# Down products of the gated experts as three f16 products, and no forced dense stretch before a step of the recurrence

## The chip, the cores and the metric

The kernel runs on one core of one Trainium2 chip. The metric is device time in microseconds, the median of several executions; the kernel before took 1439.15 us (three runs, 1434.42 to 1448.94).

## What is computed

Two decoder layers over x of 2 x 1024 tokens and 256 features. Each layer adds three results to x, each from a layer norm of x. Layer 0: causal self-attention (16 heads of 16), cross-attention to 77 context rows, and a mixture of 8 linear experts. Layer 1: a recurrence over the 1024 tokens, cross-attention, and a gated mixture of experts.

```
# the recurrence of layer 1, one step for each token
h_new = tanh(xt + h @ Wh.T + bh)

# the gated mixture of layer 1 (16 routed experts of 64, shared part of 512)
combine = zeros(S, E); combine[token, top 4 experts] = w
g = einsum('sc,ech->esh', xf, gate_w)
u = einsum('sc,ech->esh', xf, up_w)
h = silu(g) * u
hw = h * combine.T[:, :, None]
routed = einsum('esh,ehc->sc', hw, down_w)
out = x + shared_out + routed
```

The shared part has the same form without `combine`. Both parts stand side by side in the kernel as 1536 hidden features: 12 blocks of 128, of which 4 are shared and 8 routed.

## The kernel before, in words

**Chunks.** The tokens are cut into four chunks of 512 columns (256 tokens of each of the two sequences). Every layer works chunk by chunk; chunk c of a layer needs chunk c of the layer before, and the recurrence makes the history in order of time, 256 steps for a chunk.

**The recurrence.** A step is: TensorE `hi` (8 products of 2 columns, line 515), then `lo` (4 products, line 515); ScalarE `tanh` twice (line 560 to f16, line 561 to f32); VectorE `sub` (line 566), which makes the low half. `lo` waits for `sub`, `hi` of the next step for the first tanh. The 1023 steps are one chain through three engines. All other work of the layers is put between the pieces of that chain: the recurrence of chunk 0 starts when layer 0 has done its first chunk, and everything later runs beside it.

**The order.** No engine picks its work at run time. `Plan.make` writes the order of each engine before the kernel is built, from a table of costs (the number in each `st.add`), and holds a piece back that would delay the next piece of the chain by more than an allowance. Where TensorE would wait in the plan, it puts in `idle` products (line 534, up to 512 columns each, result unused). `burst` adds to that: in front of `hi` number 127, 255, ... (every `BURST_STEPS` = 128) the plan makes TensorE run for at least `BURST` = 1.7 us without a gap, with `idle` products where there is no other work.

**The gated experts.** For each of the 48 blocks (4 chunks x 12): TensorE `make` (12 products of 512 columns, line 1611, f16 pairs: high x high, low x high, high x low, for gate and up), ScalarE `tanh` (line 1619), VectorE `silu` (line 1624) and `product` (line 1632) into `hT` (a ring of three, in `tail`); for routed blocks TensorE `spread` (line 1640) and VectorE `weigh` (line 1648); then TensorE `down`: four f32 products of 256 columns (line 1663), 192 over the kernel. The program gives each f32 product to the engine as two instructions, so the profile counts 384. After 12 blocks VectorE `update` (line 1671) adds the sums to x, and `store` writes x out. The router's choice of experts is 32 short VectorE instructions for a chunk (`route`, lines 1525 to 1594). The gate and up weights are loaded in f32 and split into a high and a low f16 half in 8 parts (lines 1919 and 1924); the down weights stay in f32 in `vp`.

Of the kernel before, what the change touches and what calls it, by code (L numbers as in the profile page):

```python
# [9 lines left out]
F16 = mybir.dt.float16  # L10
# [160 lines left out]
LEAST_GAP = 0.1  # L171
BURST_STEPS = 128
BURST = 1.7
# [1245 lines left out]
class GatedExperts:  # L1419
# [7 lines left out]
    def __init__(self, st, w, ln, rank, out, room):  # L1427
        self.st, self.g, self.w, self.ln, self.room_in = st, st.g, w, ln, room.room_in
        self.xh, self.xl, self.hT, self.th = room.xh, room.xl, room.hT, room.th
        self.ex, self.sc, self.sx, self.sel, self.comb = (room.gates[:, k] for k in range(5))  # L1430
# [4 lines left out]
        self.ov = out.rearrange("(t p) d -> p t d", p=P)  # L1435
        self.s = st.sems("gat", "xh xl logits ex chain cT cph cpl cleared made th sv hm spread hc down fx stored")
        n = NK
# [27 lines left out]
        st.add("v", "gat_hc", self.weigh, n * NR, 0.66, lambda i: rank(i // NR) + 0.24, closes=lambda i: ("gat_s", i))  # L1465
        st.add("pe", "gat_down", self.down, n * MH * TC, 0.43, lambda i: rank(i // (MH * TC)) + 0.25,
               opens=lambda i: ("gat_d", i // (MH * TC), i % TC // 2) if i // TC % MH == 0 and i % 2 == 0 else None)
# [159 lines left out]
    def product(self, v, i):  # L1627
        v.wait_ge(self.s["sv"], i + 1)
        v.wait_ge(self.s["made"], 2 * i + 2)
        if i >= 3:  # L1630
            v.wait_ge(self.s["down"], i - 2)
        v.scalar_tensor_tensor(out=self.hT[:, i % 3, :], in0=self.th[:, i % 3, :], scalar=0.5 / LIFT ** 2,
                               in1=self.st.bank("gat", 2 * i + 1)[:], op0=ALU.mult, op1=ALU.mult
                               ).then_inc(self.s["hm"], 1)
# [8 lines left out]
    def weigh(self, v, i):  # L1643
# [5 lines left out]
                        ).then_inc(self.s["hc"], 1)  # L1649

    def down(self, pe, i):
        c, m, p = i // (MH * TC), i // TC % MH, i % TC
        n = MH * c + m
        o = self.st.bank("gat_d", c, p // 2)
        if m == 0 and p % 2 == 0:
            o = self.st.take(pe, "gat_d", c, p // 2)
        if i == 0:
            pe.wait_ge(*self.w.gated_in)
        if p == 0 and m < MS:
            pe.wait_ge(self.s["hm"], n + 1)  # L1660
        if p == 0 and m >= MS:
            pe.wait_ge(self.s["hc"], NR * c + m - MS + 1)
        last = pe.matmul(o[:, D * (p % 2):D * (p % 2) + D], self.hT[:, n % 3, P * p:P * p + P], self.w.wd[:, m, :],  # L1663
                         start=m == 0 and p % 2 == 0, stop=m == MH - 1, skip_group_check=True)
        if p == TC - 1:
            last.then_inc(self.s["down"], 1)

    def update(self, v, j):
        x, p = self.g.x[:, tile_of(j)[3], :], column(j) // P
        v.wait_ge(self.s["down"], MH * (j // TC + 1))  # L1670
        v.tensor_tensor(x, self.st.bank("gat_d", j // TC, p // 2)[:, D * (p % 2):D * (p % 2) + D], x, ALU.add
                        ).then_inc(self.s["fx"], 1)

# [9 lines left out]
def all_layers(g, a, out):  # L1683

    with ExitStack() as ctx:
# [24 lines left out]
        whole = tail[:].rearrange("p (k n) -> p k n", k=KD)  # L1710
        gated_room.hT = tail[:, 0:1536].rearrange("p (a n) -> p a n", a=3)
        gated_room.th = tail[:, 1536:3072].rearrange("p (a n) -> p a n", a=3)
        gated_room.xh = vp[:, 3072:3584].bitcast(F16).rearrange("p (k n) -> p k n", k=KD)
# [49 lines left out]
        wx1.ctx_in, wx1.q_in, wx1.w_in = (s["ctx1_in"], 80), (s["q1_in"], 64), (s["q1_in"], 64)  # L1763
        w.wd, w.w_hi, w.w_lo = vp[:, 0:3072].rearrange("p (m n) -> p m n", m=MH), w_parts[0:2], w_parts[2:4]
        w.gated_in = (s["w_in"], 48)
# [114 lines left out]
        def load_second(sp, i):  # L1880
# [14 lines left out]
            if i == 2:  # L1895
# [3 lines left out]
                sp.dma_start(w.cb, a["cbias"].partition_broadcast(P)).then_inc(s["w_in"], 16)  # L1899
                sp.dma_start(w.wd, a["down"].rearrange("(m p) n -> p m n", p=P)).then_inc(s["w_in"], 16)  # L1900

# [11 lines left out]
        def part(i):  # L1913
            return slice(i % 4 * HID // 4, (i % 4 + 1) * HID // 4)

        def split_high(act, i):
            j = i // 4
            act.wait_ge(s["whole_in"], 16 * (j + 1))
            act.activation(w.w_hi[j][:, :, part(i)], whole[:, :, part(i)], ACT.Copy, scale=LIFT).then_inc(s["whole_high"], 1)

        def split_low(v, i):
            j = i // 4
            v.wait_ge(s["whole_high"], i + 1)
            v.scalar_tensor_tensor(out=w.w_lo[j][:, :, part(i)], in0=whole[:, :, part(i)], scalar=LIFT,
                                   in1=w.w_hi[j][:, :, part(i)], op0=ALU.mult, op1=ALU.subtract
# [112 lines left out]
        st.add("act", "lift", lift, 1, 0.5, lambda i: -2000)  # L2038
        st.add("act", "split_high", split_high, 8, 0.8, lambda i: 1000)
        st.add("v", "split_low", split_low, 8, 0.85, lambda i: 1000)  # L2040
        st.add("v", "router", router, 2, 0.2, lambda i: 1000)
# [72 lines left out]
```

## Time and profile before

| | |
|---|---|
| median of 3 runs | 1439.15 us (1434.42 to 1448.94) |
| the profiled execution | 1442.69 us, of which the span is 1440.9 us |
| TensorE busy | 1390.5 us (96%), 19662 matmuls |
| VectorE, ScalarE busy | 814.0 us (56%), 598.6 us (42%) |
| first and last tanh of the recurrence | 223.46 us and 1299.14 us |
| mean granted TensorE clock | 0.974 |

The first 223 us are layer 0 of chunk 0 and the starts of chunk 1. Then come 1075.7 us of recurrence with other work beside it, and a tail of 141.8 us in which the recurrence is over: cross-attention of the last chunk and the gated experts of the last two. A product of TensorE is shown with its latency, so a row of one product of 256 columns says 0.27 us and a row of several in a sequence says less for each. In a row of the timeline the first number is the start, the second the time from the first start to the last end.

### The profile page before, as it was taken

How to read it: one execution, taken by the hardware profiler on the slowest of the kernel's cores; microseconds unless marked ns; L12 is line 12 of the kernel's file. 1: busy time of each engine (PE TensorE's matmuls, PEld its weight loads, DVE VectorE, ACT ScalarE, POOL GpSimd, SP SyncE). 2: the span in 40 equal slices, each digit the busy share in tenths (PEclk: the TensorE clock that was granted, in tenths of full speed). 3: DMA queues.
4: the chain of work that ended last, by engine and by line, in shares of the span. 5: the costliest groups of instructions: out<-in, count | busy, mean ns of one | idle time of the engine just before them, and what ended most of it. 6: DMA issues, size and time to landing. Idle time of an engine off the chain costs nothing.

```text
span 1440.9 us, 48024 instructions
## 1 busy us (share of the span) xinstructions
PE 1390.5 (96%) x19662; PEld 948.9 (66%) x19662; DVE 814.0 (56%) x2606; ACT 598.6 (42%) x2786; POOL 38.1 (3%) x60
## 2 busy tenths in 40 slices
PE   5699889999999999999999999999999999999998
PEld 4466346777757777775676777675766676766655
DVE  6746873278774227878841227757444553347473
ACT  2072315733424783342278864451523324332310
POOL 2000000000000000000000001000000000000000
PEclk9799989999999999999999999999989999989999
DMA  5654100030000003110000003210000200002000
GB/s 160 90 141 92 54 1 3 8 58 3 3 3 3 3 3 56 23 25 3 3 4 3 3 3 133 55 24 2 2 2 17 39 3 2 17 2 38 2 15 15
DMA packets 45469, 40.18 MB, mean 28 GB/s; under 512 B 9723, under 2 KB 44486, under 8 KB 45254
## 3 DMA queue, kind: packets, MB, share of 16 engines
q1 hardware_dynamic: 43526, 36.32, 11.4%
q8 instruction: 160, 2.62, 0.8%
q10 hardware_dynamic: 1728, 0.79, 0.5%
q14 instruction: 55, 0.45, 0.1%
HBM read 25.81 MB, written 10.80 MB: 25 GB/s over the span
## 4 chain that ended last, share of the span: by engine, by line
PE 92%; DVE 5%; DMA 1%; ACT 1%; SPq 0%; issue 0%; DVEq 0%; ACTq 0%
PE b L515 22%; PE b L1611 9%; PE b L534 8%; PE b L1663 7%; PE b L1390 6%; PE b L1003 6%; PE b L974 5%; PE b L740 4%; PE b L696 3%; PE b L919 3%; DVE mx L928 3%; PE b L1259 2%; PE b L1234 2%; PE b L651 2%; PE b L459 2%; PE b L501 1%
## 5 line engine op out<-in xcount | busy, mean ns | idle before, releaser
L515 PEld LDWEIGHTS b<-hp,whp 128*128 128x128 f16 x12276 | 476.1, 96 | 266.9 <-ACT hp L560 168.1
L515 PE MATMUL b<-hp,whp 128*128 128x2 f16 x12276 | 536.5, 165 | 1.6 <-ACT hp L560 0.3
L566 DVE TENSOR_TENSOR hp<-hist,hp 128x4 f16<-128x4 f32 x1023 | 164.7, 161 | 448.2 <-ACT hist L561 439.1
L560 ACT ACTIVATE hp<-b 128x4 f16<-128x4 f32 x1024 | 178.0, 174 | 484.4 <-PE b L515 473.5
L928 DVE TENSOR_REDUCE mx<-b 128x1 f32<-128x512 f32 (+3 forms) x304 | 187.5, 652 | 0.9 <-PE b L922 0.7
L988 ACT ACTIVATE vp<-b 128x512 f32<-128x512 f32 x288 | 171.6, 601 | 19.4 <-PE b L977 11.8
L561 ACT ACTIVATE hist<-b 128x4 f32<-128x4 f32 x1024 | 177.1, 173 | 0.0
L1611 PE MATMUL b<-vp,heads 128*128 128x512 f16 x576 | 160.1, 381 | 0.0
L534 PE MATMUL b<-whp 128*128 128x512 f16 (+6 forms) x586 | 157.9, 346 | 0.0
L919 PE MATMUL b<-heads 128*128 128x512 f16 (+3 forms) x384 | 111.8, 329 | 5.4 <-DVE mx L928 2.2
L1663 PE MATMUL b<-vp,tail 128*128 128x256 f32 x384 | 112.9, 404 | 0.0
L1390 PE MATMUL b<-we,xT 128*128 128x512 f16 x384 | 106.1, 383 | 0.0
L974 PE MATMUL b<-heads 128*128 128x256 f16 (+1 forms) x640 | 100.9, 263 | 2.0 <-DMA heads<-mp 1.8
L1003 PE MATMUL b<-vp 128*32 128x256 f32 (+1 forms) x1280 | 95.4, 370 | 0.0
L1245 ACT ACTIVATE x_pr<-b 77x512 f32<-77x512 f32 x128 | 72.8, 592 | 26.9 <-PE b L1234 26.0
L1415 DVE SCALAR_TENSOR_TENSOR x<-b,wts,x 128x256 f32<-128x256 f32 x128 | 61.8, 483 | 23.7 <-PE b L1390 18.5
L1611 PEld LDWEIGHTS b<-vp,heads 128*128 128x128 f16 x576 | 49.5, 97 | 30.4 <-ACT x_osb L645 0.5
L1663 PEld LDWEIGHTS b<-vp,tail 128*128 128x128 f32 x384 | 64.0, 191 | 8.1 <-issue 3.2
L445 POOL TENSOR_TENSOR rs<-ve,neg_half 128x2 f32<-128x2 f32 x48 | 33.8, 705 | 1334.2 <-DVE ve L439 1334.2
L974 PEld LDWEIGHTS b<-heads 128*128 128x128 f16 x640 | 55.1, 97 | 11.4 <-issue 4.7
L1619 ACT ACTIVATE tail<-b 128x512 f32<-128x512 f32 x48 | 28.7, 599 | 77.6 <-PE b L1611 77.6
L1204 DVE TENSOR_REDUCE x_nm<-b 128x4 f32<-128x308 f32 x128 | 56.8, 472 | 1.4 <-PE b L1195 0.7
(213 smaller groups left out, 1566.9 us busy)
## 6 DMA issues: line engine op xcount, KB each, us to landing
x_qs<-qx_scr SPq DMA_DIRECT2D x48, 128.0 KB
qx_scr<-xq_pair SPq DMA_DIRECT2D x16, 256.0 KB, 2.1
heads<-q_scr SPq DMA_DIRECT2D x24, 128.0 KB, 4.4
heads<-k_scr SPq DMA_DIRECT2D x36, 64.0 KB, 2.5
x<-in_x SPq DMA_DIRECT2D x8, 256.0 KB, 7.3
q_scr<-tail SPq DMA_DIRECT2D x8, 256.0 KB, 2.3
k_scr<-tail SPq DMA_DIRECT2D x8, 256.0 KB, 2.3
x_qs<-in_L_ffn_We SPq DMA_DIRECT2D x2, 1024.0 KB, 6.0
```

The lines of the kernel that those rows point to most:

```text
L515: return pe.matmul(self.z(t)[:, m], self.w.whp[:, a, k, m * P:(m + 1) * P], self.g.hp16[:, (t - 1) % 2, part, k, :], start=False, stop=Tru ...
L534: pe.matmul(self.g.b7[:, 0:min(512, columns - at)], self.w.whp[:, 0, 0, 0:P], self.w.whp[:].rearrange("p a k n -> p (a k n)")[:, 0:min(512 ...
L560: act.activation(self.g.hp16[:, t % 2, 0], self.z(t), ACT.Tanh, scale=1 / LIFT).then_inc(self.s["hi_ready"], 1)
L561: act.activation(self.g.hist[:, :, :, t % (4 * HALF)], self.z(t), ACT.Tanh, scale=1 / LIFT).then_inc(self.s["full_ready"], 1)
L566: v.tensor_tensor(self.g.hp16[:, t % 2, 1], self.g.hist[:, :, :, t % (4 * HALF)], self.g.hp16[:, t % 2, 0], ALU.subtract).then_inc(self.s[ ...
L928: v.tensor_reduce(self.mx[:, column(j) // P, head:head + heads, int(first > 0)], self.st.bank("self_first", i)[:, 0:P * n * heads].rearran ...
L974: last = pe.matmul(o[:, N * e:N * e + N], self.ks[:, b, h // 2, P * kb:P * kb + P], self.qs[:, h, QW * b + first:QW * b + QW], start=True, ...
L988: act.activation(self.pr[:, n % 2, e0:e0 + heads, first:QW], self.st.bank("self_s", i)[:, 0:N * heads].rearrange("p (e n) -> p e n", e=hea ...
L1003: last = pe.matmul(o[QD * e:QD * e + QD, QW * b + first:QW * b + QW], self.va[:, b * (S // P) + kb, at:at + QD], self.pr[:, n % 2, e, firs ...
L1390: last = pe.matmul(o[:], x[:, k, column(j):column(j) + P], self.w.we[:, wt, k, D * e:D * e + 2 * D], start=at == 0, stop=at == self.PER - 1)
L1611: last = pe.matmul(o[:], wt[:, k, m * P:(m + 1) * P], x[:, k, :], start=at == 0, stop=at == 5)
L1663: last = pe.matmul(o[:, D * (p % 2):D * (p % 2) + D], self.hT[:, n % 3, P * p:P * p + P], self.w.wd[:, m, :], start=m == 0 and p % 2 == 0, ...
```

## The change

Two parts. `BURST_STEPS` is 1024, so no `hi` of the 1023 has the forced stretch in front of it. And the down products take f16 pairs: the down weights are loaded to `heads` and split in 4 parts (ScalarE high, VectorE low), each finished hidden block is split by ScalarE (`keep_hidden`) and VectorE (`hidden_low`), and each of the 192 down products is a sum of three f16 products of 256 columns. The sum is 64 times too large (`LIFT`), which `update` takes back.

```diff
-BURST_STEPS = 128
+BURST_STEPS = 1024
...
         st.add("v", "gat_hc", self.weigh, n * NR, 0.66, lambda i: rank(i // NR) + 0.24, closes=lambda i: ("gat_s", i))
-        st.add("pe", "gat_down", self.down, n * MH * TC, 0.43, lambda i: rank(i // (MH * TC)) + 0.25,
+        st.add("act", "gat_hh", self.keep_hidden, n * MH, 0.52, of_block(0.245))
+        st.add("v", "gat_hl", self.hidden_low, n * MH, 0.6, of_block(0.246))
+        st.add("pe", "gat_down", self.down, n * MH * TC, 0.33, lambda i: rank(i // (MH * TC)) + 0.25,
...
         if i >= 3:
-            v.wait_ge(self.s["down"], i - 2)
+            v.wait_ge(self.s["hl"], i - 2)
...
+    def keep_hidden(self, act, n):
+        c, m = self.blocks[n]
+        if m < MS:
+            act.wait_ge(self.s["hm"], n + 1)
+        else:
+            act.wait_ge(self.s["hc"], NR * c + m - MS + 1)
+        if n >= 3:
+            act.wait_ge(self.s["down"], n - 2)
+        act.activation(self.hp[:, n % 3, 0, :], self.hT[:, n % 3, :], ACT.Copy).then_inc(self.s["hh"], 1)
+
+    def hidden_low(self, v, n):
+        v.wait_ge(self.s["hh"], n + 1)
+        v.tensor_tensor(self.hp[:, n % 3, 1, :], self.hT[:, n % 3, :], self.hp[:, n % 3, 0, :], ALU.subtract
+                        ).then_inc(self.s["hl"], 1)
...
-        if p == 0 and m < MS:
-            pe.wait_ge(self.s["hm"], n + 1)
-        if p == 0 and m >= MS:
-            pe.wait_ge(self.s["hc"], NR * c + m - MS + 1)
-        last = pe.matmul(o[:, D * (p % 2):D * (p % 2) + D], self.hT[:, n % 3, P * p:P * p + P], self.w.wd[:, m, :],
-                         start=m == 0 and p % 2 == 0, stop=m == MH - 1, skip_group_check=True)
+        if i == 0:
+            pe.wait_ge(self.w.s["whole_split"], 12)
+        if p == 0:
+            pe.wait_ge(self.s["hl"], n + 1)
+        for at, (h, wd) in enumerate(((0, self.w.wd_hi), (0, self.w.wd_lo), (1, self.w.wd_hi))):
+            last = pe.matmul(o[:, D * (p % 2):D * (p % 2) + D], self.hp[:, n % 3, h, P * p:P * p + P], wd[:, m, :],
+                             start=m == 0 and p % 2 == 0 and at == 0, stop=m == MH - 1 and at == 2, skip_group_check=True)
...
-        v.tensor_tensor(x, self.st.bank("gat_d", j // TC, p // 2)[:, D * (p % 2):D * (p % 2) + D], x, ALU.add
-                        ).then_inc(self.s["fx"], 1)
+        v.scalar_tensor_tensor(out=x, in0=self.st.bank("gat_d", j // TC, p // 2)[:, D * (p % 2):D * (p % 2) + D],
+                               scalar=1 / LIFT, in1=x, op0=ALU.mult, op1=ALU.add).then_inc(self.s["fx"], 1)
...
-                sp.dma_start(w.wd, a["down"].rearrange("(m p) n -> p m n", p=P)).then_inc(s["w_in"], 16)
+                sp.dma_start(wd_whole, a["down"].rearrange("(m p) n -> p m n", p=P)).then_inc(s["w_in"], 16)
...
+            if j == 2:
+                act.wait_ge(*w.gated_in)
+                act.activation(w.wd_hi[:, wd_part(i)], wd_whole[:, wd_part(i)], ACT.Copy, scale=LIFT
+                               ).then_inc(s["whole_high"], 1)
+                return
...
-        st.add("act", "split_high", split_high, 8, 0.8, lambda i: 1000)
-        st.add("v", "split_low", split_low, 8, 0.85, lambda i: 1000)
+        st.add("act", "split_high", split_high, 12, 0.8, lambda i: 1000)
+        st.add("v", "split_low", split_low, 12, 0.85, lambda i: 1000)
```

Since the plan is made anew, work moves on every engine from step 126 on (line numbers of the changed kernel from 1500 on are 2 to 34 higher: 1613 is `make`, 1642 `spread`, 1681 `down`, 1650 `weigh`, 1661 `keep_hidden`, 1665 `hidden_low`).

The first place is TensorE in front of `hi` number 127 (a row of line 515 is a `hi` of 8 products or a `lo` of 4, or both in a row of 12), before:

```order
L515 MATMUL b<-hp,whp 128x2 x8
L919 MATMUL b<-heads 128x512
L515 MATMUL b<-hp,whp 128x2 x4
L534 MATMUL b<-whp 128x512 x7
L534 MATMUL b<-whp 128x320
L515 MATMUL b<-hp,whp 128x2 x12
L1234 MATMUL b<-x_qs,x_ks 77x256 x4
```

and with the change:

```order
L515 MATMUL b<-hp,whp 128x2 x8
L919 MATMUL b<-heads 128x512
L515 MATMUL b<-hp,whp 128x2 x4
L534 MATMUL b<-whp 128x512
L534 MATMUL b<-whp 128x384
L515 MATMUL b<-hp,whp 128x2 x8
L919 MATMUL b<-heads 128x512
```

The run of 3904 idle columns in front of the step has become one of 896 columns, as in the steps around it.

The second place is TensorE in the last chunk of the gated experts, around the turning of the router's weights (line 1582, with the change 1584), before:

```order
L1611 MATMUL b<-vp,heads 128x512 x5
L1582 MATMUL b<-ident,vp 16x128 x4
L1611 MATMUL b<-vp,heads 128x512 x7
L1663 MATMUL b<-vp,tail 128x256
L1640 MATMUL b<-mp,sel_pair 128x512
L1663 MATMUL b<-vp,tail 128x256
L1640 MATMUL b<-mp,sel_pair 128x512
L1663 MATMUL b<-vp,tail 128x256 x2
L1611 MATMUL b<-vp,heads 128x512 x12
```

and with the change:

```order
L1613 MATMUL b<-vp,heads 128x512 x8
L1584 MATMUL b<-ident,vp 16x128 x4
L1613 MATMUL b<-vp,heads 128x512 x4
L534 MATMUL b<-whp 128x512 x3
L1642 MATMUL b<-mp,sel_pair 128x512 x2
L534 MATMUL b<-whp 128x512
L1642 MATMUL b<-mp,sel_pair 128x512
L534 MATMUL b<-whp 128x512 x10
L534 MATMUL b<-whp 128x256
L1681 MATMUL b<-vp,heads 128x256 x12
```

Where useful products stood between the router and the next down products, 14 idle products of 512 columns and one of 256 stand now.

The third place is VectorE in the same chunk, where routed blocks follow one another: `silu`, `product`, `weigh` before,

```order
L1624 SCALAR_TENSOR_TENSOR tail<-tail,b 128x512
L1632 SCALAR_TENSOR_TENSOR tail<-tail,b 128x512
L1648 TENSOR_TENSOR tail<-tail,b 128x512 x2
L1624 SCALAR_TENSOR_TENSOR tail<-tail,b 128x512
L1632 SCALAR_TENSOR_TENSOR tail<-tail,b 128x512
```

and with the change, with `hidden_low` behind them:

```order
L1634 SCALAR_TENSOR_TENSOR tail<-tail,b 128x512
L1650 TENSOR_TENSOR tail<-tail,b 128x512 x3
L1665 TENSOR_TENSOR heads<-tail,heads 128x512 x3
L1626 SCALAR_TENSOR_TENSOR tail<-tail,b 128x512
L1634 SCALAR_TENSOR_TENSOR tail<-tail,b 128x512
```

Each block has one VectorE instruction more in front of its down products, and three of them stand in a row behind the router.

## Rows read from the trace of the kernel before

**Rows 1.** The page, part 1: busy time, share of the span, instructions.
```profile
PE 1390.5 (96%) x19662; PEld 948.9 (66%) x19662; DVE 814.0 (56%) x2606; ACT 598.6 (42%) x2786; POOL 38.1 (3%) x60
```

**Rows 2.** Waits: engine, line, waited for, us in total, times, longest.
```profile
ACT hp L560 <- PE b L515: 473.5, 693, 2.4
DVE hp L566 <- ACT hist L561: 439.1, 687, 3.2
PEld b L515 <- ACT hp L560: 168.1, 525, 0.6
```

**Rows 3.** Groups by line and form, whole span: busy us, mean ns, idle before.
```profile
L1611 PE MATMUL b<-vp,heads 128*128 128x512 f16 x576 | 160.1, 381 | 0.0
L974 PE MATMUL b<-heads 128*128 128x256 f16 x512 | 83.4, 274 | 2.0 <-DMA heads<-mp 1.8
L1648 DVE TENSOR_TENSOR tail<-tail,b 128x512 f32<-128x512 f32 x32 | 21.6, 686 | 0.2
L1857 ACT ACTIVATE we<-x_qs 128x512 f16<-128x512 f32 x8 | 4.8, 629 | 0.0
```

**Rows 4.** Timeline of ScalarE around step 128: start, us, line.
```profile
346.79 0.17 ACT L560 ACTIVATE hp<-b 128x4 f16<-128x4 f32 x1 [0.69 <-PE b L515]
347.73 0.17 ACT L560 ACTIVATE hp<-b 128x4 f16<-128x4 f32 x1 [0.69 <-PE b L515]
349.68 0.17 ACT L560 ACTIVATE hp<-b 128x4 f16<-128x4 f32 x1 [1.70 <-PE b L515]
```

**Rows 5.** Timeline of ScalarE around step 896.
```profile
1171.14 0.17 ACT L560 ACTIVATE hp<-b 128x4 f16<-128x4 f32 x1 [0.54 <-PE b L515]
1173.06 0.17 ACT L560 ACTIVATE hp<-b 128x4 f16<-128x4 f32 x1 [1.68 <-PE b L515]
```

**Rows 6.** Timeline of TensorE, two f16 products of 256 columns in a row.
```profile
236.77 0.38 PE L974 MATMUL b<-heads 128*128 128x256 f16 x2
```

**Rows 7.** Timeline in the tail: `down` and `make` of one block, and the end.
```profile
1412.02 1.99 PE L1663 MATMUL b<-vp,tail 128*128 128x256 f32 x8
1413.85 2.75 PE L1611 MATMUL b<-vp,heads 128*128 128x512 f16 x12
...
1431.36 5.45 PE L1663 MATMUL b<-vp,tail 128*128 128x256 f32 x24
1431.92 0.69 DVE L1648 TENSOR_TENSOR tail<-tail,b 128x512 f32<-128x512 f32 x1
1436.84 1.42 DVE L1671 TENSOR_TENSOR x<-b,x 128x256 f32<-128x256 f32 x4 [4.23 <-PE b L1663]
```

**Rows 8.** Busy time by stretch: us; PE, PEld, DVE, ACT, POOL; clock, DMA, GB/s.
```profile
1277.80:1299.10 21.30, 20.97 (x383) 13.59 (x381) 10.91 (x48) 8.16 (x54) 0.69 (x1) 1.00 0.01 3
...
1380.00:1410.00 30.00, 29.89 (x142) 16.86 (x143) 22.51 (x51) 4.87 (x9) 0.00 (x0) 1.00 0.00 1
```

**Rows 9.** TensorE by stretch: busy and count, granted clock.
```profile
223.50:349.70 126.20, 126.20 (x2305) 1.00 0.12 20
...
1069.50:1072.90 3.40, 3.40 (x40) 1.00 0.02 5
1072.90:1083.20 10.30, 10.30 (x79) 0.50 0.00 0
...
1264.10:1277.70 13.60, 13.60 (x149) 0.50 0.01 2
```

**Rows 10.** Timeline of ScalarE, one step that holds other work.
```profile
946.36 0.17 ACT L560 ACTIVATE hp<-b 128x4 f16<-128x4 f32 x1 [0.24 <-PE b L515]
946.61 0.59 ACT L1245 ACTIVATE x_pr<-b 77x512 f32<-77x512 f32 x1
947.14 0.17 ACT L560 ACTIVATE hp<-b 128x4 f16<-128x4 f32 x1
```

**Rows 11.** Timeline of TensorE, step 740: its `hi` and its `lo`.
```profile
964.63 0.34 PE L515 MATMUL b<-hp,whp 128*128 128x2 f16 x8
...
1000.76 0.24 PE L515 MATMUL b<-hp,whp 128*128 128x2 f16 x4
```

More of the change, by code:

```diff
@@ L1428, in __init__ @@
         self.st, self.g, self.w, self.ln, self.room_in = st, st.g, w, ln, room.room_in
-        self.xh, self.xl, self.hT, self.th = room.xh, room.xl, room.hT, room.th
+        self.xh, self.xl, self.hT, self.th, self.hp = room.xh, room.xl, room.hT, room.th, room.hp
         self.ex, self.sc, self.sx, self.sel, self.comb = (room.gates[:, k] for k in range(5))
@@ L1435, in __init__ @@
         self.ov = out.rearrange("(t p) d -> p t d", p=P)
-        self.s = st.sems("gat", "xh xl logits ex chain cT cph cpl cleared made th sv hm spread hc down fx stored")
+        self.s = st.sems("gat", "xh xl logits ex chain cT cph cpl cleared made th sv hm spread hc hh hl down fx stored")
         n = NK
@@ L1711, in all_layers @@
         gated_room.hT = tail[:, 0:1536].rearrange("p (a n) -> p a n", a=3)
+        gated_room.hp = heads[:, 9216:10752].bitcast(F16).rearrange("p (a b n) -> p a b n", a=3, b=2)
+        wd_whole = heads[:, 6144:9216].rearrange("p (m n) -> p m n", m=MH)
         gated_room.th = tail[:, 1536:3072].rearrange("p (a n) -> p a n", a=3)
@@ L1763, in all_layers @@
         wx1.ctx_in, wx1.q_in, wx1.w_in = (s["ctx1_in"], 80), (s["q1_in"], 64), (s["q1_in"], 64)
-        w.wd, w.w_hi, w.w_lo = vp[:, 0:3072].rearrange("p (m n) -> p m n", m=MH), w_parts[0:2], w_parts[2:4]
+        w.wd_hi, w.wd_lo = (vp[:, 1536 * k:1536 * k + 1536].bitcast(F16).rearrange("p (m n) -> p m n", m=MH) for k in range(2))
+        w.w_hi, w.w_lo = w_parts[0:2], w_parts[2:4]
         w.gated_in = (s["w_in"], 48)
@@ L1914, in part, with wd_part @@
             return slice(i % 4 * HID // 4, (i % 4 + 1) * HID // 4)
+        def wd_part(i):
+            return slice(i % 4 * MH // 4, (i % 4 + 1) * MH // 4)
         def split_high(act, i):
             j = i // 4
+            if j == 2:
[3 more added lines that the diff above has]
+                return
             act.wait_ge(s["whole_in"], 16 * (j + 1))
@@ L1923, in split_low @@
             v.wait_ge(s["whole_high"], i + 1)
+            if j == 2:
+                v.scalar_tensor_tensor(out=w.wd_lo[:, wd_part(i)], in0=wd_whole[:, wd_part(i)], scalar=LIFT,
+                                       in1=w.wd_hi[:, wd_part(i)], op0=ALU.mult, op1=ALU.subtract
+                                       ).then_inc(s["whole_split"], 1)
+                return
             v.scalar_tensor_tensor(out=w.w_lo[j][:, :, part(i)], in0=whole[:, :, part(i)], scalar=LIFT,
```

## The prediction

> **What bounds the kernel now.** I read the page's busy times first: TensorE is busy 96% of the span, VectorE 56%, ScalarE 42% [rows 1]. So the cause of the time is on TensorE, but not as work alone, since it also runs idle products. The waits show the second limit: in 525 of 1023 steps TensorE's weight load waited for the first tanh, 168.1 us together; ScalarE waited 473.5 us for TensorE and VectorE 439.1 us for the second tanh [rows 2]. The kernel is in about half of its steps bound by the chain and in the other half by what TensorE was given between the pieces. In the tail (1299 to 1441 us) there is no chain; TensorE is busy 29.89 of 30 us in the stretch 1380 to 1410 [rows 8], so there each product removed counts in full unless its place is filled again.
>
> **The forced stretches.** The step into tanh 128 took 349.68 - 347.73 = 1.95 us, the one before it 0.94 us [rows 4]. The step into tanh 896 took 1.92 us [rows 5]; steps around it take 0.79. There are seven such steps (128, 256, ..., 896), the other five 1.69 to 1.94 us long. Removing them gives 1.0 us each: **-7.1 us**, all on the chain, since in the row of the order the idle columns (3904 of them at the first) are what TensorE does there.
>
> **The down products, price.** One f32 product: a block's four start at 1412.02, the next `make` at 1413.85 [rows 7], so 0.457 us each. Two f16 products of 256 columns take 0.38 us from start to end, one takes 0.274 [rows 3, 6], so 0.106 us apart, and by the `down` sequence of the change 3 x 0.108 = 0.325 us for a sum of three (0.108 is half of the 0.216 at which products of 512 columns follow: (2.75 - 0.381) / 11, [rows 3, 7]). Saved: 0.132 us a product, 192 of them, 25 us of TensorE, if nothing else moved.
>
> **The down products, place.** By the order, 96 of the 192 are before the last step, 96 behind it, before as after.
> - In steps: of the 96, 8 stand before and 10 with the change in the long stretch of step 740. That stretch is a hole in the chain, `hi` at 964.63, `lo` at 1000.76 [rows 11]; the change does not remove it, in spite of its words. In it 8 x 0.457 turn into 10 x 0.325 (-0.4) and idle columns rise by 5504 (+2.3), other products by +0.3: **+2.2 us**. The remaining 88 save 0.132 each, but only where TensorE and not the chain sets the step: half, **-5.8 us**. Nine `make` products (0.216 each) go from the steps to the tail: **-1.9 us**.
> - New work of ScalarE and VectorE in steps: 25 splits of a block on each. ScalarE's nearest row is 0.629 us (f32 to f16, 512 wide), VectorE's 0.686 [rows 3]; the weights add 4 parts of 768 columns on each, at 1.03 us by their width (0.686 x 1.5, the dearer row). These stand in the queues of tanh and `sub`. Lower bound of the cost: nothing. A step of 0.78 us holds a ScalarE instruction of 0.59 us without delay [rows 10]. Upper bound: each its whole length, 25 x (0.629 + 0.686) + 8 x 1.03 = +41 us. Between, ScalarE is idle 473.5 / 1023 = 0.46 us and VectorE 0.43 us a step [rows 2], so 25 x (0.17 + 0.26) + 4 x (0.57 + 0.60) = +15 us if every such step were a shortest one. The row of a real step is nearest to nothing, and half of the steps have more room: I take **+1 us**.
>
> Sum in the steps: -7.1 + 2.2 - 5.8 - 1.9 + 1 = -11.6 us.
>
> **The tail.** -12.7 us for 96 down products, +1.9 us for the nine `make`, and idle columns go from 14400 to 36352, which at 0.216 us for 512 are **+9.3 us**. They stand in front of places where the plan sees VectorE late: per block it has 0.686 us more (`hidden_low`). In 1380 to 1410 us VectorE works 22.51 us [rows 8]; eight more instructions make it 28.0 of 30 us, so it is nearly the bound there, and I add **+1 us** for what the plan's 0.60 us does not have of 0.686. The end: before, the last 24 instructions run from 1431.36 to 1436.8; with the change the last block's `weigh` ends at 1431.92 + 0.69 = 1432.6 [rows 7], the splits follow (0.63 + 0.69 and some 0.15 of signals: 1434.1), then 12 products of 0.108 (1435.4 and latency 0.17, so 1435.6): **-1.2 us**, of which the products before (1431.36 + 24 x 0.108 = 1433.95) hide the rest. But that gain is already in the -12.7, so it isn't added. The four `update` instructions at the very end are chained by one another's 0.36 us and grow by 0.07 each: +0.2. Sum in the tail: -0.3 us.
>
> Total **-12 us**: span and execution go from 1440.9 and 1442.69 us to 1429 and 1430.7. The profiled execution is 3.5 us above the median of the runs, within their spread of 14.5 us, so I take the same -12 off the median: **1427 us**.
>
> **The clock, where row and rule part.** The granted clock was at its lower level, 1.2 GHz, from 1072.9 to 1083.2 and from 1264.1 to 1277.7 us (and twice more, for 6.8 us each) although TensorE was busy all of these stretches, 10.30 of 10.30 us in the first [rows 9]. In the second it gave 149 products in 13.6 us, 11.0 a us; right behind it 383 in 21.3 us, 18.0 a us [rows 8, 9]: 5.3 us lost. Before that first fall it had no gap either, 3.40 of 3.40 us, but only 40 matmuls in it, 11.8 a us against 18.3 a us in the first 126 us of steps [rows 9]. The Trainium skill, TensorE: Matmul & The Clock Gate, section Loop structure matters more than you think, has the clock fall where TensorE waits long between groups of matmuls; by that rule a kernel that never stops TensorE pays nothing, and neither do the stretches removed here: the clock's term of the sum would be 0 by the rule. By the rows it can be something. I take 0 all the same, from other rows: from 223.5 to 349.7 us no forced stretch had yet run, and the clock stayed at 2.4 GHz (1.00) throughout [rows 9].
>
> **Rivals.**
> 1. *The saved time is given back in waits* (the chain takes all that isn't a forced stretch). For it: 525 steps wait for tanh. Against it: the other half do not. Only the -7.1 remain, with +2.2 in the hole and +1 for queues: 1439 - 4 = 1435 us. Chance 0.22.
> 2. *The plan uses all of it.* If the counted columns set the time everywhere, the steps give -12.7 (96 products) - 1.9 (`make`) and, for idle columns, which fall from 227776 to 223424, -1.8, so -16.4; the tail -1.5: 1421 us. For it: TensorE is busy 99.8% in the steps. Against: busy counts latency. Chance 0.24.
> 3. *The clock falls instead* (slower than before). The mechanism is thin work that no dense stretch interrupts: TensorE in front of steps 128 to 896. If the clock fell once in each of the seven spans from which a stretch is gone, at 5.3 us each, +37 us: 1464 us. It decides from the third such fall on (3 x 5.3 is more than 12). For it: four falls in the rows with TensorE busy. Against: none in the first 126 us, without a stretch. Chance 0.08.
> 4. *The new queue work delays the chain by the average shortage*, +15 for +1: 1441 us, no change. It would need the splits to stand in the shortest steps. Chance 0.06.
>
> My forecast, -12 us give or take 5, has 0.40.
>
> **How the numbers follow.** The predicted time is the likeliest case's, 1427 us, its own range 1421 to 1433. The range for 8 in 10 reaches on the fast side past rival 2 to one clock stretch less than before (1421 - 5 - 2 = 1414), on the slow side over rival 1 and up to rival 4's middle, with one clock stretch more (1435 + 5): 1440. A measurement of this kernel can tell about 1% (14.4 us), so faster is below 1424.8 us: most of rival 2 (0.20) and the faster half of the forecast's own spread, with runs that differ by 14.5 us (0.21): 0.41. Slower is above 1453.5 us: 0.08 of rival 3 and 0.02 of the others: 0.10. The rest, 0.49, is within 1%.
>
> **What the changed profile would show.** Steps into tanh 128, 256, ... of 0.8 to 1.1 us (burst term right); a step 740 of some 39 us; `down` in groups of 12 that take 1.3 us up to the next `make`, against 1.83 (price right); mean of VectorE's new line near 0.69 and of ScalarE's near 0.63 us; first to last tanh near 1064 us, against 1075.7 (sum in the steps); from the last tanh to the end about 141.5 us (tail). More than 45 us at the lower clock would speak for rival 3, steps around the new splits longer by 0.2 us or more for rival 4. The prediction is wrong if the tail grows by more than 3 us through VectorE, or if the order's new packing lets waits of other kinds (transfers, stores of the cross-attention) stand in front of a step.

## The result, and the profile after

The changed kernel took 1423.83 us, the median of four runs (1419.4 to 1426.8), beside 1437.69 us for the kernel before: a ratio of 0.9877, 95% interval 0.9836 to 0.9918. The forecast was 1427 us; its range, 1414 to 1440, holds the time. The whole interval lies below 1, so the direction was right. The size was forecast too small: by the ratio the kernel gained 17.7 us (0.0123 x 1437.69), by the two medians alone 13.9 us, where the forecast had 12. At equal clock, as explained with the table below, it is 18 us.

The page of the changed kernel, part 1 (the row of [rows 1] is its counterpart):

```profile
span 1422.8 us, 48634 instructions
PE 1374.9 (97%) x19892; PEld 938.5 (66%) x19892; DVE 845.1 (59%) x2658; ACT 626.7 (44%) x2838; POOL 37.9 (3%) x60
```

TensorE stays the bound; VectorE works 31 us and ScalarE 28 us more, mainly for the splits. The waits (engine, line, waited for: us in total, times, longest), beside [rows 2]:

```profile
ACT hp L560 <- PE b L515: 433.6, 672, 1.5
DVE hp L566 <- ACT hist L561: 402.1, 673, 3.2
PEld b L515 <- ACT hp L560: 170.8, 537, 0.4
```

ScalarE and VectorE wait 40 and 37 us less for the chain, while TensorE's own wait for tanh hardly moves (168.1 before). The steps became shorter because TensorE had less to do between them, not because the chain itself did. Groups by line and form (busy us, mean ns, idle before), beside [rows 3]:

```profile
L1681 PE MATMUL b<-vp,heads 128*128 128x256 f16 x576 | 78.7, 272 | 0.0
L1665 DVE TENSOR_TENSOR heads<-tail,heads 128x512 f16<-128x512 f32 x48 | 32.5, 686 | 6.2 <-ACT heads L1661 6.1
L1689 DVE SCALAR_TENSOR_TENSOR x<-b,x 128x256 f32<-128x256 f32 x16 | 6.2, 418 | 3.4 <-PE b L1681 3.4
L1661 ACT ACTIVATE heads<-tail 128x512 f16<-128x512 f32 x48 | 30.0, 630 | 23.6 <-DVE tail L1650 17.2 <-DVE tail L1634 6.4
```

The prices of the split instructions are those of the forecast (forecast 0.686 and 0.629 us, measured 0.686 and 0.630). The `update` has not grown by the forecast's 0.07 us: it takes 0.418 us, as before.

ScalarE's timeline around step 128 and step 896 of the changed kernel (start, us, line), the counterparts of [rows 4, 5]:

```profile
349.42 0.17 ACT L560 ACTIVATE hp<-b 128x4 f16<-128x4 f32 x1 [0.69 <-PE b L515]
350.35 0.17 ACT L560 ACTIVATE hp<-b 128x4 f16<-128x4 f32 x1 [0.69 <-PE b L515]
...
1161.67 0.17 ACT L560 ACTIVATE hp<-b 128x4 f16<-128x4 f32 x1 [0.54 <-PE b L515]
1162.49 0.17 ACT L560 ACTIVATE hp<-b 128x4 f16<-128x4 f32 x1 [0.57 <-PE b L515]
```

The step into tanh 128 takes 0.93 us, it took 1.95; the one into tanh 896 takes 0.82, it took 1.92. Now the stretches of the span, from the starts of line 560 in each trace (the start of a trace varies by 5 us between kernels with the same first 200 us, and means nothing):

| | before | changed | difference | forecast |
|---|---|---|---|---|
| tanh 0 to tanh 640, no gated experts in them | 634.3 | 632.7 | -1.7 | -5.1 |
| the long step 740 | 36.75 | 39.26 | +2.5 | +2.2 |
| the other steps from 640 on | 404.6 | 384.3 | -20.3 | -8.7 |
| last tanh to the end | 141.8 | 141.4 | -0.4 | -0.3 |

The forecast's column is its own sum, cut at step 640: five and two forced stretches (-5.1, -2.0), then -5.8, -1.9 and +1. One row is wrong by much: the steps with gated experts. The clock is in these rows too. Both profiles have 37.5 us at the lower clock between the first and the last tanh, but before has all of it from step 640 on, and the changed kernel has 3.4 us in front of it and 34.1 us behind. At the forecast's rate (5.3 us lost in 13.6) that moves 1.3 us from one row to the other: at equal clock the first row is -3.0 and the third -19.0. The second profile of the changed kernel, without a fall in front of step 640, says 631.2 us for the first row, -3.1.

### The profile page after: what moved, and what is told of

It reads as the page before. It is cut to its first block, busy times and chain, and to the rows that moved or that the text cites. A ratio compares the mean times of both kernels' runs of the same rounds, so it can differ in the third digit from the quotient of the medians.

```text
span 1422.8 us, 48634 instructions
## 1 busy us (share of the span) xinstructions
PE 1374.9 (97%) x19892; PEld 938.5 (66%) x19892; DVE 845.1 (59%) x2658; ACT 626.7 (44%) x2838; POOL 37.9 (3%) x60
## 4 chain that ended last, share of the span: by engine, by line
PE 92%; DVE 4%; DMA 1%; ACT 1%; issue 1%; SPq 0%; DVEq 0%; ACTq 0%
PE b L515 23%; PE b L1613 9%; PE b L534 8%; PE b L1390 6%; PE b L1003 6%; PE b L974 5%; PE b L740 5%; PE b L1681 5%; PE b L919 4%; PE b L696 3%; DVE mx L928 3%; PE b L1259 3%; PE b L1234 2%; PE b L651 2%; PE b L459 2%; PE b L501 1%
## 5 line engine op out<-in xcount | busy, mean ns | idle before, releaser
L534 PE MATMUL b<-whp 128*128 128x512 f16 (+6 forms) x624 | 168.8, 347 | 0.0
L1681 PE MATMUL b<-vp,heads 128*128 128x256 f16 x576 | 78.7, 272 | 0.0
L1613 PEld LDWEIGHTS b<-vp,heads 128*128 128x128 f16 x576 | 50.0, 97 | 29.8 <-issue 0.7
L974 PEld LDWEIGHTS b<-heads 128*128 128x128 f16 x640 | 55.0, 97 | 11.4 <-issue 4.6
L1681 PEld LDWEIGHTS b<-vp,heads 128*128 128x128 f16 x576 | 51.2, 97 | 10.1 <-issue 2.3
L919 PEld LDWEIGHTS b<-heads 128*128 128x128 f16 x384 | 36.5, 97 | 29.2 <-DVE mx L928 22.2
```

Of the source, the lines that this page charges most:

```text
L534: pe.matmul(self.g.b7[:, 0:min(512, columns - at)], self.w.whp[:, 0, 0, 0:P], self.w.whp[:].rearrange("p a k n -> p (a k n)")[:, 0:min(512 ...
L919: last = pe.matmul(o[:, at:at + P * n], self.qs[:, h, column(j):column(j) + P], self.ks[:, b, h // 2, P * first:P * first + P * n], start= ...
L974: last = pe.matmul(o[:, N * e:N * e + N], self.ks[:, b, h // 2, P * kb:P * kb + P], self.qs[:, h, QW * b + first:QW * b + QW], start=True, ...
L1613: last = pe.matmul(o[:], wt[:, k, m * P:(m + 1) * P], x[:, k, :], start=at == 0, stop=at == 5)
L1681: last = pe.matmul(o[:, D * (p % 2):D * (p % 2) + D], self.hp[:, n % 3, h, P * p:P * p + P], wd[:, m, :], start=m == 0 and p % 2 == 0 and ...
```

## The experiments

The runs of one kernel differ by more than most of the effects, and each run lists its mean granted clock. Over all 163 executions in the 14 rows of the table (the changed kernel has two) straight lines with one slope fit with a scatter of 1.5 us: 1.08 us less for each 0.001 of clock. The last two columns are worked out with it: a kernel's time at a clock of 0.977, against the kernel before at the same clock. Where medians and this column differ, the kernel ran at another mean clock. The runs were made in three groups, each beside its own runs of before; these come out at 1438.3, 1437.5 and 1437.2 us at a clock of 0.977, so a difference between kernels of different groups is good to about 1 us and no better.

| kernel | median, us | ratio to before, 95% | mean clock | at 0.977, us | difference |
|---|---|---|---|---|---|
| before (60 runs) | 1436.7 to 1445.1 | | 0.9747 | 1437.7 | |
| changed (4 runs) | 1423.83 | 0.9877 [0.9836, 0.9918] | 0.9735 | 1419.7 | -18.0 |
| changed, again | 1422.83 | 0.9899 [0.9863, 0.9934] | 0.9730 | 1420.0 | -17.7 |
| no stretches, f32 | 1434.0 | 0.9946 [0.9916, 0.9976] | 0.9775 | 1433.8 | -3.9 |
| stretches, f16 pairs | 1419.75 | 0.9855 [0.9813, 0.9897] | 0.9808 | 1422.9 | -14.8 |
| f16 products alone, old order | 1414.5 | 0.9834 [0.9788, 0.9879] | 0.9757 | 1413.9 | -23.8 |
| splits alone | 1442.33 | 1.0031 [0.9997, 1.0065] | 0.9764 | 1442.8 | +5.1 |
| stretches every 64 steps | 1433.78 | 0.9958 [0.9923, 0.9992] | 0.9742 | 1429.6 | -8.1 |
| router filled | 1424.87 | 0.9890 [0.9844, 0.9937] | 0.9742 | 1420.5 | -17.2 |
| router and bias filled | 1416.58 | 0.9836 [0.9792, 0.9879] | 0.9835 | 1423.4 | -14.3 |
| measured durations in the table | 1432.0 | 0.9925 [0.9887, 0.9962] | 0.9685 | 1420.7 | -17.0 |
| allowance 0.35 | 1413.81 | 0.9812 [0.9757, 0.9867] | 0.9745 | 1412.0 | -25.7 |
| no low half | 1422.24 | 0.9869 [0.9814, 0.9923] | 0.9710 | 1415.8 | -21.9 |
| both fills, measured durations | 1419.13 | 0.9845 [0.9793, 0.9898] | 0.9820 | 1424.8 | -12.9 |

### The two parts apart

Without the forced stretches, everything else as before:

```diff
-BURST_STEPS = 128
+BURST_STEPS = 1024
```

> The kernel before with the forced stretches alone taken out (f32 down products stay). Theory A (the forecast's term): seven steps shorter by 1.0 us each, all on the chain: 7 us less, 1430 to 1431 us. Rival B (given back): in the changed kernel the seven steps are 7.0 us shorter together, but steps 0 to 640, where five of them lie and nothing else of the change does, took 632.6 us against 634.3 us, only 1.7 us less; then this kernel gains 2 to 3 us, 1435 us. Rival C (clock): without the stretches the granted clock falls more often; slower than before, with more than 45 us at the lower clock.

7.8 us less by the ratio, 3.9 at equal clock. Steps 0 to 640 took 631.3 us against 634.3: -3.0, where the five steps with a stretch became 4.9 us shorter (4.5 us together, 9.4 before). The plan that is made anew lengthened the other steps by 1.9 us. It gave back more at the end: from the last tanh on the kernel took 146.0 us against 141.8, though no stretch ever stood there. Step 740 is 2.2 us shorter, and the other steps from 640 on are 6.8 us shorter, of which the clock has 4.0 (27.3 us at the lower clock against 37.5). The four places make -3.0 - 2.2 - 2.8 + 4.2 = -3.8 us. Rival B is what happened at equal clock; the 7 us of theory A are within the interval of the ratio only with the clock's help.

The changed kernel with the stretches back:

```diff
-BURST_STEPS = 1024
+BURST_STEPS = 128
```

> The changed kernel with the forced stretches put back (every 128 steps). Theory A: what the forecast left for the f16 products, -5 us against before (1433 us). Theory D (the f16 products are worth more than forecast, since an f32 product costs 0.515 us between the pieces of a step and not 0.457): the changed kernel's -17.7 us less the 2 to 7 us of the stretches, so -11 to -15 us: 1423 to 1427 us.

-14.8 us at equal clock: theory D. And -3.9 - 14.8 = -18.7 against -18.0 and -17.7 for both: the parts add up within the 1 us of the groups. The places do not add up so simply: with the stretches the tail takes 135.7 us and step 740 takes 42.34, in the changed kernel 141.4 and 39.26. Taking the stretches out lengthens the tail here too, by 5.7 us. By its median alone this kernel is as fast as the changed one or faster, and that is the clock: 0.9808 against 0.973.

### What the f16 products are worth

The order of before, with the products exchanged and nothing added on the other engines:

```diff
-        last = pe.matmul(o[:, D * (p % 2):D * (p % 2) + D], self.hT[:, n % 3, P * p:P * p + P], self.w.wd[:, m, :],
+        for at in range(3):
+            last = pe.matmul(o[:, D * (p % 2):D * (p % 2) + D], self.w.w_lo[at // 2][:, at % 2, P * p:P * p + P],
```

> The order of the kernel before, instruction for instruction, with each f32 down product replaced by three f16 products of 256 columns on other resident operands; no splits of the hidden block, no new plan. It leaves out the use of the hidden block and of the down weights. Theory A (0.132 us saved a product, half of it lost in steps): 1 + 5.8 in the steps and 12.7 in the tail, -19.5 us: 1418 us. Theory D (in steps a product starts behind products of 2 columns, and takes 0.515 us; the three take 0.325): 88 x 0.19 + 1 + 12.7, up to -30 us where TensorE sets every such step: 1408 to 1413 us; first to last tanh 12 to 18 us shorter than 1075.7.

-23.8 us at equal clock, between the two. By stretches of the profile: tail 132.0 us against 141.8 (-9.8), step 740 -0.75, the other steps from 640 on 386.0 against 404.6 (-18.6). In those steps this run had 17 us less at the lower clock than the profiled run of before (20.5 against 37.5), worth 6.6 us at the 5.3 us lost in 13.6 of the forecast. That leaves -12.0 us for 88 products: 0.136 us each, where the forecast put 0.066. A comparison step by step needs no correction, since both kernels have the same order: the steps in which the clock was at its upper level in both profiles, with 85 of the products in 73 of them, became 11.4 us shorter, 0.134 us for a product; the 271 other steps changed by 0.0 us in sum.

The rows say why. TensorE's timeline in a step of before:

```profile
963.91 0.34 PE L515 MATMUL b<-hp,whp 128*128 128x2 f16 x8
964.11 0.68 PE L1663 MATMUL b<-vp,tail 128*128 128x256 f32 x2
```

The `lo` or `hi` behind it starts at 964.63 [rows 11], 0.52 us after the product did. In a step of the changed kernel:

```profile
1033.13 0.49 PE L1681 MATMUL b<-vp,heads 128*128 128x256 f16 x3
1033.46 0.44 PE L515 MATMUL b<-hp,whp 128*128 128x2 f16 x12
```

0.33 us. Of the single f32 products in steps that have a chain product behind them, the median of this distance is 0.515 us. The difference lies between the two instructions of a pair. In a stream of f32 products each instruction starts 0.216 us after the one before. The first pair of a stream is further apart, the more so the shorter the product in front of it: 0.299 us behind products of 2 columns, which follow one another by 0.025 us, 0.258 behind 154 columns, 0.218 behind 256 and 0.216 behind the 512 of `make`. That fits a weight load (0.19 us for f32, 0.097 for f16) that only a long enough product in front can cover. Behind `spread` (48 rows), where the load starts with its own product and not ahead of it, it is 0.320:

```profile
1412.02 1.59 PEld L1663 LDWEIGHTS b<-vp,tail 128*128 128x128 f32 x8 [0.23 <-issue]
```

So the forecast's 0.457 was (0.320 + 7 x 0.216) / 4; a block's four products behind `make` take 0.432 each. Saved in a step is therefore up to 0.19 us and not 0.132, and of at most 88 x 0.19 = 16.7 us the chain takes back some 5 us, not half of 11.6.

### What the splits cost

The kernel before, with `keep_hidden` and `hidden_low` added and waited for, f32 products as they were:

```diff
+        st.add("act", "gat_hh", self.keep_hidden, n * MH, 0.52, of_block(0.245))
+        st.add("v", "gat_hl", self.hidden_low, n * MH, 0.6, of_block(0.246))
...
-        if p == 0 and m < MS:
-            pe.wait_ge(self.s["hm"], n + 1)
+        if p == 0:
+            pe.wait_ge(self.s["hl"], n + 1)
```

> The kernel before (forced stretches stay, down products in f32) with the two split instructions of each hidden block added and waited for; their results are not used. Theory A (the forecast): +1 us in the steps and about +10 us in the tail, where idle columns go from 14400 to 36416: 1448 to 1450 us. Rival E (new work in the queues of tanh and sub delays the chain by its shortage): +11 us more in the steps, first to last tanh 1087 us or more: 1460 us.

+5.1 us at equal clock, less than either. First to last tanh 1074.9 us against 1075.7, the tail 144.2 against 141.8. But this profile has 27.3 us at the lower clock between the tanhs and before has 37.5, worth 4.0 us, so at equal clock the steps are 3.2 us longer. The new work in the queues of tanh and `sub` costs about 3 us there, more than the forecast's 1 and far less than the 15 of its rival 4, which is out; how much of the 3 is a wait in a queue and how much another order was not taken apart. And idle columns that a plan shows in the tail are not all lost time: they went up by 22016, or 9.3 us, and the tail by 2.4 us. They partly stand where TensorE would have waited, or where other work was done earlier.

The changed kernel without VectorE's half:

```diff
-        st.add("v", "gat_hl", self.hidden_low, n * MH, 0.6, of_block(0.246))
...
-        for at, (h, wd) in enumerate(((0, self.w.wd_hi), (0, self.w.wd_lo), (1, self.w.wd_hi))):
+        for at, (h, wd) in enumerate(((0, self.w.wd_hi), (0, self.w.wd_lo), (0, self.w.wd_hi))):
```

> The changed kernel without VectorE's split instruction: the third product takes the high half of the hidden block again, so the low half is left out of the sum. TensorE has the same products. Idle columns in the tail 24064 against 36352 (-5.2 us), in the steps 225280 against 223424 (+0.8). The forecast's terms for this instruction, +9.3 + 1 us of idle columns and VectorE time in the tail and up to +1 in the steps, give -5 to -8 us at equal clock; if the instruction delays the chain (rival 4 of the forecast), -12 us or more.

4 us less than the changed kernel at equal clock, just short of the 5 to 8: the VectorE instruction costs about what the other experiment gave for both. But the gain is not where it was expected: the tail, with 12288 idle columns fewer, took 143.1 us against 141.4, and step 740 took 33.96 against 39.26. The parts put together: -23.8 + 5.1 = -18.7, where f16 pairs as a whole gave -14.8. In step 740 alone f16 pairs as a whole gave +5.6 us where the two parts gave -0.8 and -0.4. The remaining 4 us (splitting the weights, another packing) were not taken apart.

### The forced stretches and the clock

> The changed kernel once more, beside the others of this group. In the runs so far a kernel's time falls by 1.1 us for each 0.001 of mean granted clock, and the changed kernel had 0.9735 in four runs, the one with f16 products and the forced stretches 0.9808. If that difference belongs to the kernels, this comes out at 1423 to 1424 us again with 0.973 to 0.975; if it was the luck of four runs, at 1419 to 1421 us.

It repeats: -17.7 us at equal clock, clock 0.973.

```diff
-BURST_STEPS = 1024
+BURST_STEPS = 64
```

> The changed kernel with forced stretches twice as often as before, every 64 steps (15 of them; plan made anew). Theory A: 1.0 us each without getting anything back: +15 us on the changed kernel. Theory B (part of a stretch is given back by the plan, as 5.1 us in five steps became 3.0 us net in steps 0 to 640): +9 us at equal clock. Theory C (stretches hold the clock up): mean clock 0.98 or more and no more than +3 us.

9.6 us slower than the changed kernel at equal clock, for 15 stretches: 0.64 us each, theory B. Its mean clock is 0.9742. With stretches the means are 0.9747 (before), 0.9808 and 0.9742, without 0.9775, 0.9735 and 0.9730: no order in it. By these means forced stretches at a distance of 64 or 128 steps do not hold the clock, and the fall of rival 3 (slower than before) did not come.

Where the clock falls in the changed kernel (TensorE by stretch: busy and count, granted clock), beside [rows 9]:

```profile
904.50:911.30 6.80, 6.59 (x100) 0.50 0.25 73
911.30:1105.90 194.60, 193.84 (x2831) 1.00 0.05 9
1105.90:1119.50 13.60, 13.60 (x134) 0.50 0.06 20
1252.60:1262.90 10.30, 10.30 (x139) 0.50 0.01 2
```

And what TensorE did before the second and the third of these falls:

```profile
1101.33 0.29 PE L63 MATMUL b<-first,vp 128*128 128x16 f16 x6
1101.73 0.52 PE L515 MATMUL b<-hp,whp 128*128 128x2 f16 x12
1102.11 0.30 PE L63 MATMUL b<-first,vp 128*128 128x16 f16 x6
1102.52 0.52 PE L515 MATMUL b<-hp,whp 128*128 128x2 f16 x12
...
1249.20 0.24 PE L515 MATMUL b<-hp,whp 128*128 128x2 f16 x4
1249.38 0.69 PE L698 MATMUL b<-bo,one_row 1*128 1x256 f32 x2
1250.00 0.45 PE L515 MATMUL b<-hp,whp 128*128 128x2 f16 x12
```

Router products of 16 columns, and bias products with one active row. That is a pattern and not yet a cause, but it is in all profiles: in each of the eleven whose router products have nothing put behind them at least one fall from step 640 on, 17 in all, starts 0.1 to 2.4 us after such a product. Idle products behind the first:

```diff
             for k in range(KD)]).then_inc(self.s["logits"], 1)
+        self.fill(pe)
...
+        gated.fill = lambda pe: rnn.idle(pe, 512)
```

> The changed kernel with one idle product of 512 columns behind each of the 16 groups of router products (16 columns wide) of the gated experts; same order otherwise. Theory F (the clock falls behind thin work, and the falls at 904 and 1106 us follow the router's products): these two falls, 6.8 and 13.7 us long, are gone or shorter, mean clock up by 0.005, 16 x 0.216 = 3.5 us at most are paid and 5 to 8 us come back: 1419 to 1422 us against 1423.8. Rival: the falls come where they came, +2 to +3.5 us.

Neither fall behind router products is in this profile, but others are (880.5, 1023.8 and 1245.7 us, 37.5 us together), and the mean clock is 0.9742: the falls went elsewhere, and theory F fails for the router alone. And behind both:

```diff
         if last_k:
             last.then_inc(self.s["y"], 1)
+        if k == KD:
+            self.fill(pe)
```

> As the kernel before in this list, and one idle product of 512 columns behind each of the 16 bias products (one active row) in the outputs of the second cross-attention. Theory F: the falls near 1252 and 1269 us go too, mean clock 0.985 or more, at most 3.5 us more are paid: 1416 to 1422 us. Rival: clock as before, +5 to +7 us.

Mean clock 0.9835 in six runs, from 0.979 to 0.988, where the changed kernel has 0.973; at equal clock 3.4 us are paid, in sum it is 6.3 us faster than the changed kernel beside it. In its profile (same columns) the last fall lies at 1040 us, and none behind it:

```profile
1040.20:1050.40 10.20, 10.20 (x118) 0.50 0.01 2
1050.40:1418.00 367.60, 363.71 (x4724) 1.00 0.07 15
```

### The plan itself

```diff
-        st.add("act", "gat_hh", self.keep_hidden, n * MH, 0.52, of_block(0.245))
-        st.add("v", "gat_hl", self.hidden_low, n * MH, 0.6, of_block(0.246))
+        st.add("act", "gat_hh", self.keep_hidden, n * MH, 0.6, of_block(0.245))
+        st.add("v", "gat_hl", self.hidden_low, n * MH, 0.68, of_block(0.246))
```

> The changed kernel with the measured durations in the plan's table for the two split instructions (0.60 for 0.52 on ScalarE, 0.68 for 0.60 on VectorE); plan made anew. Idle columns in the steps go from 223424 to 220416 (-1.3 us), in the tail from 36352 to 42432 (+2.6 us). If the columns count: +1 us at equal clock. If the tail's waits for VectorE were real and not in the plan: -1 us or less. A difference of more than 3 us at equal clock would mean that the packing of a plan is worth as much as a term of the forecast.

+0.7 to 1.0 us at equal clock, as the columns say; the median is 9 us worse through a mean clock of 0.9685. The same table with both fills:

> The kernel with both idle fills and the measured durations in the table: the candidate for a faster version. If the fills hold the clock whatever the order, mean clock 0.983 or more and 1416 to 1418 us as before; if the clock of the fill kernel was the luck of its order, 0.975 and 1424 us.

Mean clock 0.982 in place of 0.9685, at 4.1 us paid; the median, 1419.13 us, is short of the 1416 to 1418 expected. The fills raised the clock in a second order too. Why they do is open. In none of the three profiles with a filled router does a fall follow router products, but in the profile of this one (same columns) a fall does follow the filled bias products:

```profile
1246.00:1263.10 17.10, 17.10 (x219) 0.50 0.01 2
```

Falls near 1024 us, behind neither of the two, are in all three. And an order alone moves the mean as far: without any fill it was 0.9685 in one kernel and 0.9808 in another. And the allowance:

```diff
-LATE = 0.3
+LATE = 0.35
```

> The changed kernel with the plan's allowance for delaying the chain at 0.35 in place of 0.30: same work, another packing. Idle columns in the steps 207872 against 223424 (-6.6 us), in the tail 41408 against 36352 (+2.1 us). If columns count: -4 us at equal clock; if a later chain takes it back: 0 to +3 us.

-7.7 us against the changed kernel at equal clock, twice what the columns gave. Its steps up to 640 are 15.7 us longer (648.4; 4 us of that are the clock's, with 13.7 us at the lower level in them against 3.4), step 740 is 15.6 us shorter (23.7) and the tail 5.5 us shorter (135.9): more work beside the chain early, less behind it. This is the fastest kernel of all, 1413.81 us and 0.9812 [0.9757, 0.9867] of the one before; the changed kernel's intervals overlap with it in the upper part. It was not combined with the fills.

## Why the prediction was right, and where not

- **The bound.** Right. TensorE's work between the pieces of the chain set the steps, and TensorE set the tail.
- **Forced stretches.** 1.0 us each was measured right: the seven steps take 6.2 us where they took 13.2. That this was "all on the chain" was wrong: the kernel gains 3.9 us at equal clock, since the new plan lengthens other steps and the tail. The forecast had numbers that say so: outside step 740 the idle columns of the steps fall by 4352 + 5504 = 9856, 4.2 us, not 7.1.
- **Price of a product.** 0.325 us for three was right (twelve take 1.31 us up to the next `make`, 1372.61 to 1373.92 in the tail below). 0.457 us for the f32 product was read from one block of the tail, behind `spread`; it is 0.432 behind `make` and 0.515 in most steps. So the saving was put too low in the steps and too high in the tail (-12.7 us forecast, -9.8 with the products alone exchanged).
- **Place.** This is the step that failed: "only where TensorE and not the chain sets the step: half, -5.8 us". The order of before with the cheaper products gave -12.0 in the same steps: both the share was too low (some 0.7 of the saving stays) and the price (up to 0.19 us a product for 0.132). In 25 of 63 places the new plan even puts two products in a slot of 0.65 us, where one of 0.52 was. The half was taken from the count of steps in which the weight load waits, but f32 products stand in the others: in the kernel before, from step 640 on and without the long one, the 76 steps that hold one had a mean of 1.21 us and only 8% of them were among the shortest (up to 0.80 us), of the 306 others, with a mean of 1.02 us, 25% were. The steps with the products were mostly TensorE's. The other steps from 640 on came out at -20.3 us (-19.0 at equal clock) where -8.7 were forecast; the products explain 6 us of the difference, and what remains, some 4 us, belongs to the new order and was not taken apart. So first to last tanh took 1056.2 us and not the 1064 forecast.
- **The hole** at step 740: +2.5 us against +2.2. Its length belongs to the order: it went from 23.70 to 42.34 us over the kernels of the table.
- **Queue work**: +1 us taken; when the splits alone were added, first to last tanh grew by 3.2 us at equal clock. The low end of the bounds was the right one, but 1 was too little.
- **The tail**: -0.4 us, where -0.3 was forecast, and that is luck. The terms were -12.7 for the products, +10.3 for idle columns and VectorE, +1.9 for `make`, +0.2 for the `update`, and nothing for the stretches. The runs gave -9.8 for the products, +2.4 for the splits, and +4.2 or +5.7 for taking the stretches out; with the same 1.9 for `make` that is -1.3 to +0.2. TensorE's timeline of the changed kernel there:

```profile
1372.61 1.47 PE L1681 MATMUL b<-vp,heads 128*128 128x256 f16 x12
1373.92 2.75 PE L1613 MATMUL b<-vp,heads 128*128 128x512 f16 x12
...
1388.65 0.81 PE L534 MATMUL b<-whp 128*128 128x512 f16 x3
1389.43 0.59 PE L1642 MATMUL b<-mp,sel_pair 48*128 48x512 f16 x2
1389.95 0.39 PE L534 MATMUL b<-whp 128*128 128x512 f16 x1
1390.28 0.39 PE L1642 MATMUL b<-mp,sel_pair 48*128 48x512 f16 x1
1390.60 2.44 PE L534 MATMUL b<-whp 128*128 128x512 f16 x11
1392.87 1.47 PE L1681 MATMUL b<-vp,heads 128*128 128x256 f16 x12
...
1417.23 1.47 PE L1681 MATMUL b<-vp,heads 128*128 128x256 f16 x12
```

Between 1388.65 and 1392.87 there are 3.4 us of idle products in front of the next `down`, as much as six blocks of `down` were forecast to save (0.53 us each). The plan put them there because of VectorE, whose first split of these blocks ends only at 1391.72 + 0.69 = 1392.4 us:

```profile
1389.92 1.88 DVE L1650 TENSOR_TENSOR tail<-tail,b 128x512 f32<-128x512 f32 x3
1391.72 1.89 DVE L1665 TENSOR_TENSOR heads<-tail,heads 128x512 f16<-128x512 f32 x3
```
At the very end VectorE's split of the last block ends at 1416.44 + 0.69 = 1417.13 us and `down` starts at 1417.23, as the forecast had it (0.1 us of signal):

```profile
1416.44 0.69 DVE L1665 TENSOR_TENSOR heads<-tail,heads 128x512 f16<-128x512 f32 x1 [0.70 <-ACT heads L1661]
```

- **The clock.** Taken at 0, and the change moved the mean from 0.9747 to 0.9735 and 0.9730, within its scatter. The Trainium skill, TensorE: Matmul & The Clock Gate, section Loop structure matters more than you think, looks for falls where TensorE waits long between matmuls. This trace does not agree: TensorE is busy 20.00 of the 20.00 us before the fall at 1252.6 us and 10.30 of 10.30 in it, and 19.67 of 20.00 us before the one at 1105.9. The measurement decides. Many of the falls here follow thin products, and two kernels in which idle products were put behind these had a mean clock higher by 0.0105 and 0.0135 than the same order without them. That the thin products cause the falls is not shown.
- **Rivals.** Nearest is rival 2 (all counted columns count, 1421 us, chance 0.24); the measured time lies between it and the forecast.

## What to carry to other kernels

Read the price of an instruction where it stands: here a f32 product behind products of two columns costs 0.08 us more than one behind 256 or 512 columns (0.515 against 0.43), and the rows fit a weight load that has nothing to hide behind. Do not halve a saving by the share of steps that wait; ask in which steps the saved work stands. Do not take a sum for right because it came out: the tail's did, with three terms off by 3 to 8 us. And where an order is planned, compare at equal granted clock and count a new packing as a change of its own: three settings of the planner with the same work differed by 8.7 us here.

## What was not expected of the hardware

The spread of the runs is the clock's. Executions of the kernel before went from 1424.82 to 1452.09 us, and the mean granted clock accounts for all but 1.5 us of scatter. TensorE never stopped in most of the stretches at 1.2 GHz (13.60 of 13.60 us busy at 1105.9 in the changed kernel, 10.30 of 10.30 at 1252.6). Thirty-two idle products of 512 columns, 6.9 us of TensorE's time, were worth more than they cost in both orders in which they were tried (3.4 us paid at equal clock and some 11 us back through the clock; 4.1 and some 15). Whether fewer would do, and what they act on, stays open.
